# Two-layer AdaLN transformer with attention and experts: VectorE empties the job and expert banks before it takes the maximum of the scores

## What is computed

```python
h = _layernorm(x, axis=-1) * (1 + ca) + sa
scores = jnp.einsum('bhqd,bhkd->bhqk', q, k) / jnp.sqrt(jnp.float32(d))
attn = jax.nn.softmax(scores, axis=-1)          # layer 0 adds a bias by distance to the scores
ctx = jnp.einsum('bhqk,bhkd->bhqd', attn, v)
x = x + ga * (ctx @ Wo.T + bo)
h = _layernorm(x, axis=-1) * (1 + cb) + sb
topk_w, topk_i = jax.lax.top_k(h @ router_weight, K)
x = x + gb * experts(h, topk_w, topk_i)         # layer 1: plus a gated shared expert
```

## Time and profile before

| | us |
|---|---|
| median of 3 runs | 1912.3 |
| lowest, highest | 1907.36, 1919.51 |
| time of the profiled execution | 1904.66 |
| span of the profiled execution | 1902.9 |

### The profile page before, as it was taken

How to read it: one execution, slowest core, us unless ns; L and a number is a source line. 1 busy time by engine, 2 the same in 40 slices (tenths; PEclk the granted TensorE clock), 3 DMA queues, 4 the chain that set the end, 5 groups by cost and what they waited for, 6 DMA issues and landing times.

```text
span 1902.9 us, 44348 instructions
## 1 busy us (share of the span) xinstructions
PE 1492.8 (78%) x13810; PEld 904.3 (48%) x13810; DVE 1364.7 (72%) x4301; ACT 1083.5 (57%) x2436; POOL 997.5 (52%) x1283
## 2 busy tenths in 40 slices
PE   2778888888999888889898889989998988525540
PEld 1234444434555555555555555555555555524440
DVE  6668888877888888888888888888878775302211
ACT  1367766766777666666666566666665664212220
POOL 1222224543444466756665666646654556657746
PEclk9989989988999999999999999999999999757775
DMA  6674344534555455555454554545554433324432
GB/s 205 158 200 99 94 98 96 118 99 101 127 126 136 120 128 137 137 133 127 114 130 124 127 130 115 125 116 139 132 125 110 119 98 94 95 67 136 127 97 61
DMA packets 381604, 229.43 MB, mean 121 GB/s; under 512 B 28847, under 2 KB 370161, under 8 KB 380867
## 3 DMA queue, kind: packets, MB, share of 16 engines
q1 hardware_dynamic: 352675, 186.72, 39.5%
q0 software_dynamic: 16384, 33.59, 6.0%
q10 hardware_dynamic: 12320, 6.29, 1.1%
HBM read 122.44 MB, written 103.98 MB: 119 GB/s over the span
## 4 chain that ended last, share of the span: by engine, by line
PE 41%; DVE 22%; issue 14%; POOL 13%; ACT 4%; another core or an unknown queue 3%; DMA 2%; SPq 0%; ACTq 0%; POOLq 0%; DVEq 0%
PE ps_s L1125 8%; PE ps_job L996 8%; DVE mx L1531 8%; POOL y_in L634 5%; PE ps_q L965 3%; PE ps_q L984 2%; PE ps_q L947 2%; PE ps_job L1099 2%; PE ps_q L977 2%; POOL slot_dram L617 2%; PE ps_job L1091 1%; DVE ln_st L1296 1%; PE ps_job L1017 1%; PE ps_job L1030 1%
## 5 line engine op out<-in xcount | busy, mean ns | idle before, releaser
L1531 DVE TENSOR_REDUCE mx<-ps_s 128x2 f32<-128x512 f32 x1024 | 686.9, 682 | 167.3 <-PE ps_s L1125 147.6
L794 ACT ACTIVATE prob<-ps_st 128x512 f32<-128x512 f32 x1024 | 599.3, 595 | 156.4 <-PE ps_st L1131 124.7
L1125 PE MATMUL ps_s<-k_stk,q_stk 51*128 51x256 bf16 x2048 | 407.1, 285 | 110.9 <-DVE mx L1531 69.8
L1131 PE MATMUL ps_st<-q_stk,k_stk 53*128 53x256 bf16 x2048 | 403.7, 282 | 1.7 <-ACT prob L794 1.6
L996 PE MATMUL ps_job<-prob,v_ext 128*32 128x256 f32 x4096 | 289.8, 402 | 26.4 <-issue 17.0
L634 POOL DMA_INDIRECT y_in<-y_dram,slot x256 | 251.6, 983 | 98.4 <-issue 58.1
L1125 PEld LDWEIGHTS ps_s<-k_stk,q_stk 51*128 51x128 bf16 x2048 | 118.1, 95 | 373.6 <-issue 186.4
L617 POOL DMA_INDIRECT slot_dram<-h_row,slot x256 | 257.3, 1005 | 61.6 <-issue 58.6
L727 ACT ACTIVATE o_sb<-ps_job 128x256 f32<-128x256 f32 x256 | 98.1, 383 | 225.8 <-PE ps_job L996 173.5
L657 POOL TENSOR_TENSOR qk_rest<-qk_f,qk_part 128x512 f32<-128x512 f32 x64 | 74.0, 1156 | 278.9 <-ACT qk_part L822 277.9
L996 PEld LDWEIGHTS ps_job<-prob,v_ext 128*32 128x32 f32 x4096 | 116.7, 112 | 134.5 <-issue 45.3
(11 more groups left out here) (205 smaller groups left out, 2810.9 us busy)
## 6 DMA issues: line engine op xcount, KB each, us to landing
part_dram<-qk_part SPq DMA_DIRECT2D x128, 192.0 KB
q_stk<-part_dram SPq DMA_DIRECT2D x128, 192.0 KB
k_stk<-part_dram SPq DMA_DIRECT2D x128, 192.0 KB
h_blk<-slot_dram SPq DMA_DIRECT2D x88, 256.0 KB
y_dram<-y_sb SPq DMA_DIRECT2D x80, 256.0 KB
part_dram<-qk_part SPq DMA_DIRECT2D x128, 128.0 KB
mod_in<-row_dram SPq DMA_DIRECT2D x64, 192.0 KB
part_dram<-qk_part SPq DMA_DIRECT2D x128, 64.0 KB
```

Source lines behind the costliest of these rows:

```text
L794: sc.activation(prob[:, (k ^ 1) % 8, :], ps_st[k % 2][:], ACT.Exp).then_inc(exp_done, 1)
L1125: mm = pe.matmul(ps_s[j % 2][:, t * S:(t + 1) * S], q_stk[us.tri][r0:r0 + R_BIAS, hp, t * P:(t + 1) * P], k_stk[us.tri][r0:r0 + R_BIAS, hp ...
L1131: mm = pe.matmul(ps_st[k % 2][:, t * S:(t + 1) * S], k_stk[ut.tri][r1:r1 + R_MAX, hp, t * P:(t + 1) * P], q_stk[ut.tri][r1:r1 + R_MAX, hp, ...
L1531: dve.tensor_reduce(mx[:, hp // 4, :, 4 * par + hp % 4], ps_s[j % 2][:].rearrange("p (t s) -> p t s", s=S), AX_X, ALU.max).then_inc(max_do ...
```

## The change

In each step VectorE now does the clips, gated products, splits, normalising, attention product and shared products first, and the maximum behind them. The instructions, their operands and their waits are the same; TensorE's order is the same.

```diff
--- before.py
+++ after.py
@@ -1522,14 +1522,6 @@
             for step in range(FIRST, STEPS):
                 if step == SETUP:
                     setup()
-                u, j = head_at(step, 0)
-                if u:
-                    hp, par = j // 2, j % 2
-                    dve.wait_ge(s_mm, u.count(16, j + 1))
-                    if u.has(1) and j % 8 == 0:
-                        dve.wait_ge(mx_split, u.count(4, 2 * (j // 8) - 2))
-                    dve.tensor_reduce(mx[:, hp // 4, :, 4 * par + hp % 4], ps_s[j % 2][:].rearrange("p (t s) -> p t s", s=S),
-                                      AX_X, ALU.max).then_inc(max_done, 1)
                 q = quad_at(step, 3)
                 if q:
                     quad_clip(q)
@@ -1557,6 +1549,14 @@
                     u = at(step, after)
                     if u and u.layer == 1:
                         shared_act(u, c)
+                u, j = head_at(step, 0)
+                if u:
+                    hp, par = j // 2, j % 2
+                    dve.wait_ge(s_mm, u.count(16, j + 1))
+                    if u.has(1) and j % 8 == 0:
+                        dve.wait_ge(mx_split, u.count(4, 2 * (j // 8) - 2))
+                    dve.tensor_reduce(mx[:, hp // 4, :, 4 * par + hp % 4], ps_s[j % 2][:].rearrange("p (t s) -> p t s", s=S),
+                                      AX_X, ALU.max).then_inc(max_done, 1)
                 for part in range(3):
                     u = at(step, 74 + part // 2)
                     if u:
```

## The result

The changed kernel takes 1976.46 us, median of 4 runs (1972.38 to 1980.80), against 1912.53 us before, median of 4 (1907.36 to 1919.51): ratio 1.0332, 95% interval 1.0291 to 1.0373. It is 3.3% slower. That is the outcome that was forecast; the predicted 1,962 us is 14 us short.

What follows compares the result with a forecast made beforehand. VectorE and TensorE were taken to hand the lead to each other, neither bounding alone. Layer 0's 34.9, layer 1's 12.8 and 6.4, and clips' 4.5 make 58.6 us on 1,904.7; forecast 1,962 us, range 1,926 to 1,990.

Steps and rivals of the forecast that it cites:

- two hand-overs: VectorE passes the lead to TensorE at places 2 and 4, TensorE passes it back at place 10; neither bounds alone.
- Place 2: Normalising goes ahead of the maximum, so place 4's scores start 0.49 us later; 32 units of layer 0, 15.7 us.
- does not get the drain's earlier end back: At place 4, the normalising ending earlier would not let TensorE's value product follow its scores any sooner.
- this one hides it: In layer 1, the 0.40 us delay from place 3's shared products would hide the 0.49 us delay from place 2.
- Place 10: Maximum no longer fits into the attention product's wait; top two and place 12's value product 0.60 us later, layer 0 only.
- Places 0, 8 and 15: Splits and the other half's normalising delay the maximum by up to 0.5 us, ending in place 4's wait; counted zero.
- Clips: Clipping of experts' gates at place 1 in layer 0's quads: 9 counted at 0.5 us, together 4.5 us.
- Shared products: Layer 1's shared expert, 0.40 us each: 32 times at place 3 (12.8 us), 16 at place 13 (6.4 us).
- The sum: All terms of both layers together, 58.6 us, added to the profiled 1,904.7 us; stated as 1,962 us, chance 0.62.
- rival D: Worse than the sum: waits stack and TensorE's clock falls more often; 1,986 us, or 1,990 with layer 0's clips; chance 0.12.
- Rivals B and C: B: slack takes up most of the delay, 1,920 us, chance 0.19. C: drain waits vanish, faster, 1,869 us, chance 0.07.
- sign of being wrong: TensorE's idle time before place 4's scores not growing, or layer 1's rounds shortening as shared products fill VectorE's waits.

Runs made afterwards that it cites:

- att: The kernel before, with the attention product of place 10 alone put ahead of the maximum of its step; ratio 1.0061.
- norm2: The kernel before, with the normalising (places 15 and 2) alone put ahead of the maximum, run a second time; ratio 1.0112.
- rows67_l0: The kernel before, with norm_rows (four VectorE instructions) moved two steps later for layer 0's units alone; ratio 0.9919.
- after_fill: The changed kernel, with extra useless matmuls in TensorE's pauses at places 2 and 4 of layer 0; ratio 1.0262.
- fill: The kernel before, with extra useless matmuls in TensorE's pauses at places 2 and 4 of layer 0; ratio 0.9931.
- norm_fill: The kernel before, with the normalising ahead of the maximum and extra matmuls at places 2 and 4 of layer 0; ratio 1.0098.
- norm_fill2: The kernel before, with the normalising ahead of the maximum and extra matmuls in layer 0, run again on another chip; ratio 1.0107.
- split: The kernel before, with the splits of the maxima (places 0 and 8) alone put ahead of the maximum; ratio 1.0055.

## Why the prediction came true, point by point

- **What bounds the kernel**: two hand-overs, between which one engine or the other leads. Confirmed from both sides: work put ahead of a hand-over lengthens the undisturbed round (`att` 0.65, `norm2` 0.41 us), work taken away shortens it (`rows67_l0`, 0.57 us).
- **Place 2, 0.49 us per unit**: the delay ahead of place 4 is 0.49 us as said (idle 1.24 to 1.73 us in `norm2`), but that 0.41 arrive in the round is the balance of two things that the prediction excluded: 0.19 us from place 15 on top, and 0.28 us back at place 4, where TensorE "does not get the drain's earlier end back". The term was 15.7 us; the runs gave 21.5 to 24 us. The surplus is in layer 0 and goes with a lower clock. Whether "this one hides it" holds in layer 1 stays open: the delay arises there too, and what is left of it is 0, 2 or 12 us by the pair of runs.
- **Place 10, 0.60 us per unit**: right in size, 0.65 us, in rounds without quads. Multiplied by all 32 units it was too much; where quads are, the rounds show no clear difference. The term was 19.2 us, the run gave 11.7. Nothing for layer 1 was right: the interval between the scores of places 11 and 12 grows by 0.06 us there.
- **Places 0, 8 and 15, nothing**: right for place 0 in layer 0 (0.04 us are left of 0.33), wrong for place 15 (0.19 us, above) and for place 8 in layer 1; the splits cost 10.6 us in all. The argument was made at places 2 and 4 of layer 0 and carried over to place 8, where no wait of place 4 follows. And the split doesn't cost "its own length, under 0.5 us": beside GpSimd's product it takes 0.84 us.
- **Clips**: 4.5 us counted, 7.5 measured.
- **Shared products**: 19.2 us counted, 6 measured. The delay at places 5 and 15 was taken for a delay of the round.
- **The sum**: 58.6 us, measured 63.9 by the medians and 69.8 by the profiled executions' spans. About 8 us of the distance from 1,962 to the measured 1,976 are the starting point: the sum was added to the 1,904.7 us of the profiled execution, not to the median. The sum is near in part by luck: terms too large (attention product, shared products) and too small (normalising, splits, clips) cancel; the absolute misses add up to some 40 us. For undisturbed rounds of layer 0 it holds well, 1.02 us for 1.09. In layer 1 I had 0.74 with the clips; compared unit by unit where both rounds are at the upper clock level, `after_fill` is 0.71 us longer than `fill` on one chip (22 rounds) and the changed kernel 0.59 longer than the kernel before (18 rounds).
- **The clock** (in rival D, not in the sum): it did fall, 0.93 to 0.87. Of the 50.9 us in the first half, rounds at the upper level explain 20 x 1.02 + 12 x 0.73 = 29.2 (the 0.73 is a difference of medians over few rounds; unit by unit it is 0.45). The other 21.7 us go with 58 us more at the lower level, for which the estimate above gives 21 us. The Trainium skill, TensorE: Matmul & The Clock Gate, in its section on PSUM-queue depth-cycling, reports a kernel in which small pauses between groups of matmuls make the clock swing. The traces here agree, with 0.93 falling to 0.87 as the pauses grew and rising to 0.97 in `fill`, where they were filled. How much of it is left in the total is open, see above.
- **Rivals B and C**: out. No single part was without a cost; slack takes up two thirds of the shared products' term, but not the change. Waits for the normalising fell from 14.6 to 0.6 us and those for the attention product are no longer listed; waits for the maxima grew by 101.9 us. The rule "Evacuate promptly" of the Trainium skill (PSUM — Partial Sum Buffer, summary of rules for kernel authors) gives the size of PSUM as its reason and doesn't decide between two banks that both wait to be emptied. Here the measurement says: first the one for which TensorE stands still.
- **What would show it**: seen were the longer waits for the maximum (272.2 us), the attention product's wait in one block (1.82 us), the scores of place 4 directly behind their maximum, VectorE's unchanged busy time, 1.02 us per undisturbed round of layer 0 and 21.5 / 32 = 0.67 per round of layer 1, and lower waits for drains. Not as said: TensorE's busy time grew by 28.4 us, and over all rounds of layer 0 it is 50.9 / 32 = 1.59 us each. Neither sign of being wrong was seen: the idle time before the scores of place 4 grew, by 0.19 us, and the rounds of layer 1 did not get shorter.

## What to carry to other kernels

When two engines take turns in leading, look for the places where the lead passes and count only what stands between them; work that is cheap elsewhere costs much of its length there (0.41 us of 0.49, 0.65 for 0.60), and taking it away pays (0.57 of 1.05). If an instruction waits for another engine and the one ahead of it fits into that wait, swapping the two costs the whole length of the latter where the waiting engine leads from there on, though no work was added. A matmul row without idle time is no proof of slack: look at the row of its weight load, and at how long ago the maximum that frees the bank had ended (0.06 us here). And ask of an instruction that moves what it will run beside on the other engines.

## What was not expected of the hardware

- The same kernel took 1,846 us on one chip and 1,923 us on two others, 4% apart, more than the whole change. The difference isn't spread evenly. Undisturbed rounds of layer 0 are equally long (18.10 us in `fill` on the faster chip); the rounds of layer 1 took 813.8 us in `norm_fill` and 852.6 in `norm_fill2`, the same kernel, and the part behind the last scores 325 to 327 us in all four profiles of the faster chip and 345 to 361 us in the others. The cause wasn't examined.
- After two pauses of 1.28 and 1.43 us TensorE's clock stood at its lower level for most of 10.2 us, through which it was busy for all but 0.03 us. Its own work took so much longer that VectorE waited in turn.
- A subtraction of 128 x 16 elements on VectorE (`mx_part`) took 0.72 us at 1106.41, where its mean in the kernel before is 0.18. In all 35 such cases of `split` and of the changed kernel it started beside a GpSimd product of 128 x 256 elements and ended 0.03 us behind it. VectorE's maximum, which reads a PSUM bank, ran beside the same product in the kernel before and took its usual 0.68 us.
